# Last state-space stage of a decoder kernel: causal mask as a minimum on VectorE, exponential in place, score products on GpSimd

## What is computed

```python
zxbcdt = hidden_states @ W_in               # z: 4096, x: 4096, B: 128, C: 128, dt: 64
xbc = silu(causal_conv1d(xbc, conv_w) + conv_b)      # 4 taps
dt = softplus(dt + dt_bias)
dA_cs = cumsum(dt * A, axis=tokens)
diff = dA_cs[i] - dA_cs[j]                  # per sequence, per head, 128x128
L = exp(where(j <= i, diff, -inf))
Y = einsum('bcign,bcjgn,bcijgh,bcjghp->bcighp', C, B, L, dt * x)
y = (Y + D * x) * silu(z)
out = (y * rsqrt(mean(y * y) + eps) * norm_w) @ W_out
```

## Time and profile before

| | |
|---|---|
| median of 3 runs | 1987.97 us (1985.36 to 1990.80) |
| profiled execution | 1988.18 us |
| its span, first to last instruction | 1986.4 us |
| TensorE busy | 1718.8 us, 87% of the span |
| VectorE busy | 1181.7 us, 59% |
| ScalarE busy | 922.8 us, 46% |
| GpSimd busy | 443.1 us, 22% |
| mean granted TensorE clock | 0.945 of full |
| the loop over pairs | about 1200 to 1625 us of the span |

### The profile page before, as it was taken

The page is one execution under the profiler, slowest core; times in us unless marked ns, Lnnn a source line. Parts: engine busy times, 40 slices in busy tenths (PEclk is TensorE's granted clock), DMA queues, the critical chain, the costliest instruction groups (busy, mean ns, idle before and its releaser), DMA issues. The chain is left out here.

```text
span 1986.4 us, 37376 instructions
## 1 busy us (share of the span) xinstructions
PE 1718.8 (87%) x13974; PEld 1341.0 (68%) x13974; DVE 1181.7 (59%) x2340; ACT 922.8 (46%) x1876; POOL 443.1 (22%) x497
## 2 busy tenths in 40 slices
PE   7976756789999899977667878999999997999898
PEld 4765643469999755653456756777777785888666
DVE  3675568556555622225653477888888865666632
ACT  2344466336655521212144355667667653555432
POOL 1020010123333131221300123445455441000200
PEclk9998977899999999998779899999999998999999
DMA  2020000401000082221000000101011003111000
GB/s 97 2 88 2 3 29 1 138 9 33 24 24 24 19 354 39 46 32 63 13 1 3 26 25 17 33 24 32 25 31 32 24 16 118 33 32 32 1 1 22
DMA packets 27104, 77.86 MB, mean 39 GB/s; under 512 B 2928, under 2 KB 14832, under 8 KB 24560
## 3 DMA queue, kind: packets, MB, share of 16 engines
q1 hardware_dynamic: 22912, 71.17, 10.5%
q0 software_dynamic: 4080, 5.13, 1.6%
HBM read 63.01 MB, written 13.28 MB: 38 GB/s over the span
## 5 line engine op out<-in xcount | busy, mean ns | idle before, releaser
L2446 DVE SCALAR_TENSOR_TENSOR arena<-bank,arena 128x508 f32<-128x508 f32 (+2 forms) x204 | 151.5, 743 | 28.5 <-ACT arena L2442 16.1
L217 PE MATMUL bank<-const 128*128 128x256 f32 (+1 forms) x244 | 101.7, 531 | 37.2 <-PEq L65 37.2
L2572 PE MATMUL bank<-L3a_wo,L3a_y_gated 128*128 128x256 f32 x512 | 124.0, 386 | 0.0
L2800 DVE TENSOR_TENSOR L3a_decays<-L3a_decays,L3a_cb_masked 128x512 f32<-128x512 f32 x128 | 94.7, 802 | 44.0 <-ACT L3a_decays L2684 44.0
L2684 ACT ACTIVATE L3a_decays<-bank 128x512 f32<-128x512 f32 x128 | 66.1, 604 | 98.1 <-PE bank L2546 98.1
L2599 PE MATMUL bank<-L3a_xnT_high,L3a_w_high 128*128 128x512 f32 x256 | 106.3, 415 | 1.5 <-ACT L3a_decays L2684 1.5
L2572 PEld LDWEIGHTS bank<-L3a_wo,L3a_y_gated 128*128 128x128 f32 x512 | 92.4, 190 | 17.5 <-issue 7.3
L2599 PE MATMUL bank<-L3a_xnT_high,L3a_w_low 128*128 128x512 f32 x256 | 100.6, 393 | 0.0
L2599 PE MATMUL bank<-L3a_xnT_low,L3a_w_high 128*128 128x512 f32 x256 | 100.4, 392 | 0.0
L217 PEld LDWEIGHTS bank<-const 128*128 128x128 f32 x244 | 44.1, 208 | 64.4 <-issue 64.4
L1863 PE MATMUL bank<-L1f_experts,xnT 128*128 x184 | 84.6, 603 | 2.3 <-DVE xnT L1965 2.3
(11 more groups left out here) (592 smaller groups left out, 4762.5 us busy)
## 6 DMA issues: line engine op xcount, KB each, us to landing
arena<-in_L3p SPq DMA_DIRECT2D x32, 388.0 KB, 3.0
L1f_experts<-in_L1f SPq DMA_DIRECT2D x8, 1536.0 KB, 17.3
arena<-in_L1x SPq DMA_DIRECT2D x18, 384.0 KB, 3.0
arena<-in_L3x SPq DMA_DIRECT2D x18, 384.0 KB, 3.0
arena<-in_L0f SPq DMA_DIRECT2D x1, 4224.0 KB, 13.8
arena<-in_L3f SPq DMA_DIRECT2D x1, 4055.0 KB, 12.8
rows_sent<-L1a_blank SPq DMA_DIRECT2D x1, 2967.0 KB, 11.2
xnT<-rows_sent SPq DMA_DIRECT2D x23, 129.0 KB, 2.0
```

The lines of the kernel that those rows point to most:

```text
L217: self.nc.tensor.matmul(self.k.ps[bank][:, 0:width], self.k.ident, self.k.const[:, 0:width], start=True, stop=True)
L2446: return nc.vector.scalar_tensor_tensor(dst[:, :, d:], psum[:, :, 0:P - d], wcol, dst[:, :, d:], ALU.mult, ALU.add)
L2572: mm = nc.tensor.matmul(ps[g // 2][:, (g % 2) * C:(g % 2 + 1) * C], yg[:, o, g * P:(g + 1) * P], wo[:, o, :], start=False, stop=False, ski ...
L2800: nc.vector.tensor_tensor(d, d, cbm[:, 4 * half:4 * half + 4, :].rearrange("p b t -> p (b t)"), ALU.mult).then_inc(S["dec_ready"], 1)
```

## The change

- The mask leaves TensorE: `later`, `ident_r` and the four mask matmuls are gone, and each difference matmul starts its bank itself.
- VectorE's `bound` takes the place of `weigh`: for each of four banks the minimum of the differences in PSUM and `highest`, a 128x128 table (1e30 where allowed, -1e30 elsewhere) repeated for four sequences, written to `dec` in SBUF. It now gives `diff_read`, and waits for `y_psum` where the exponentials did.
- ScalarE's exponentials run in place in `dec`, after `diff_read`, and give the new `exp_ready`.
- `weigh` moves to GpSimd, to the end of its pass, behind the sum of squares; the first pair's is done in pass 1, ahead of the second's.

```diff
--- before.py
+++ after.py
@@ -2413,7 +2413,7 @@
         da_src = da[:, :, :].rearrange("p (f m) (a q h) -> p f m a q h", f=2, q=2, h=2)
         dax_dst = dax[:, :, :].rearrange("p a (h f r q m) -> p a h f r q m", h=2, f=2, r=4, q=2)
         ROWS = [[(h, f, r) for h in range(2) for f in range(2) for r in own] for own in ((0, 1), (2, 3))]
-        identr, later = st.sb("ident_r", [P, P], F32R), st.sb("later", [P, 4, P], F32R)
+        highest = st.sb("highest", [P, P])
         lrow = st.sb("diff_left", [P, 2, P], F32R)
         rrow = st.sb("diff_right", [P, 4, P], F32R)
         dec = st.sb("decays", [P, 2, 2, NB, P])
@@ -2425,7 +2425,7 @@
         S = {n: st.sem(n) for n in (
             "dt_psum", "zdt", "abs_dt", "exp_dt", "exp1_dt", "log_dt", "bc_psum", "bc_first", "bc_conv",
             "bc_ready", "cb_psum", "cb_ready", "da_ready", "z_psum", "x_psum", "z_read", "x_scaled", "x_read",
-            "x_conv", "x_ready", "xt_psum", "xt_read", "diff_psum", "diff_read", "dec_ready",
+            "x_conv", "x_ready", "exp_ready", "xt_psum", "xt_read", "diff_psum", "diff_read", "dec_ready",
             "y_psum", "y_read", "y_ready", "pair_small", "wo_ready", "out_done", "sq_ready", "sq_added",
             "ms_psum", "zero_set", "dve_step", "d_ready", "x_high", "x_low", "w_high",
             "w_split", "dA_rows", "dA_rows_act", "cs_psum", "cs_copy", "cs_high", "cs_merged", "cs_left", "cs_rows", "steps_ready", "slot_read", "mask_set")}
@@ -2539,12 +2539,9 @@
                             pe.wait_ge(S["xt_read"], j * 2 - 1 + n)
                         else:
                             pe.wait_ge(S["y_read"], j * 2 - 5 + n)
-                        nc.tensor.matmul(bank("d", n)[:, :], identr[:, :], later[:, :, :].rearrange("p m t -> p (m t)"),
-                                         start=True, stop=False)
-                    for n in range(4):
                         g = slice(32 * n, 32 * n + 32)
                         nc.tensor.matmul(bank("d", n)[:, :], lrow[g, s, :], rrow[g, :, :].rearrange("p m t -> p (m t)"),
-                                         start=False, stop=True).then_inc(S["diff_psum"], 1)
+                                         start=True, stop=True).then_inc(S["diff_psum"], 1)
 
                 def make_y(pe, j, o):
 
@@ -2630,7 +2627,6 @@
 
                 pe.sem_inc(S["out_done"], SLOT_FREE)
                 pe.wait_ge(S["x_low"], 1)
-                pe.wait_ge(S["mask_set"], 2)
                 passes(pe, pair, tail)
 
             @block.scalar
@@ -2678,11 +2674,9 @@
                 def exponents(act, j, s):
                     d4 = dec[:, s, :, :, :].rearrange("p h b t -> p (h b t)")
                     for n in range(4):
-                        act.wait_ge(S["diff_psum"], j * 4 + n + 1)
-                        if not early(j):
-                            act.wait_ge(S["y_psum"], j * 2 - 2)
-                        nc.scalar.activation(d4[:, n * HALF:(n + 1) * HALF], bank("d", n)[:, :],
-                                             ACT.Exp).then_inc(S["diff_read"], 1)
+                        act.wait_ge(S["diff_read"], j * 4 + n + 1)
+                        d = d4[:, n * HALF:(n + 1) * HALF]
+                        nc.scalar.activation(d, d, ACT.Exp).then_inc(S["exp_ready"], 1)
 
                 def squares(act, j, o):
 
@@ -2738,8 +2732,7 @@
                 ln.vector(dve)
                 step = Chain(dve, S["dve_step"])
                 nc.vector.memset(zero[:, :], 0.0).then_inc(S["zero_set"], 1)
-                nc.vector.tensor_copy(identr[:, :], k.ident).then_inc(S["mask_set"], 1)
-                nc.vector.tensor_copy(later[:, :, :], over(k.c["causalT"], 4)).then_inc(S["mask_set"], 1)
+                nc.vector.tensor_scalar(highest[:, :], k.c["causalT"], 2.0, BIG, ALU.mult, ALU.add).then_inc(S["mask_set"], 1)
                 dve.wait_ge(S["x_high"], 1)
                 nc.vector.tensor_tensor(xl[:, :, :], xnT[:, :, :], xh[:, :, :].bitcast(F32),
                                         ALU.subtract).then_inc(S["x_low"], 1)
@@ -2791,15 +2784,16 @@
                         nc.vector.tensor_scalar(csl[:, t], csl[:, t], rows[:, 2:3], rows[:, 3:4], ALU.mult,
                                                 ALU.add).then_inc(S["cs_rows"], 1)
 
-                def weigh(dve, j, s):
+                def bound(dve, j, s):
 
                     for n in range(4):
                         h, half = n // 2, n % 2
-                        d = dec[:, s, h, 4 * half:4 * half + 4, :].rearrange("p b t -> p (b t)")
-                        dve.wait_ge(S["diff_read"], j * 4 + n + 1)
-                        nc.vector.tensor_tensor(
-                            d, d, cbm[:, 4 * half:4 * half + 4, :].rearrange("p b t -> p (b t)"),
-                            ALU.mult).then_inc(S["dec_ready"], 1)
+                        dve.wait_ge(S["diff_psum"], j * 4 + n + 1)
+                        if not early(j):
+                            dve.wait_ge(S["y_psum"], j * 2 - 2)
+                        nc.vector.tensor_tensor(dec[:, s, h, 4 * half:4 * half + 4, :],
+                                                bank("d", n)[:, :].rearrange("p (b t) -> p b t", b=4),
+                                                over(highest[:, :], 4), ALU.min).then_inc(S["diff_read"], 1)
 
                 def skip(dve, j, o):
 
@@ -2826,7 +2820,7 @@
                     first = is_first(j)
                     step.restart()
                     if not first:
-                        weigh(dve, j, s)
+                        bound(dve, j, s)
                     for half in range(2):
                         dve.wait_ge(S["x_scaled"], j * 2 + half + 1)
                         p3 = bank("x", half)[:, :].rearrange("p (b t) -> p b t", b=4)
@@ -2849,7 +2843,8 @@
                                                 bank("t", half)[:, :].rearrange("p (b h d) -> p b h d", b=4, h=2),
                                                 along(dtc[:, s, bs, :], HD), ALU.mult).then_inc(S["xt_read"], 1)
                     if first:
-                        weigh(dve, j, s)
+                        dve.wait_ge(S["mask_set"], 1)
+                        bound(dve, j, s)
                     else:
                         gate(dve, j, 1 - s)
 
@@ -2894,6 +2889,18 @@
                     pool.wait_ge(S["sq_ready"], j + 1)
                     nc.gpsimd.tensor_tensor(sqsum, sqsum, ysq, ALU.add).then_inc(S["sq_added"], 1)
                     pool.wait_ge(S["sq_added"], j + 1 + SLOT_FREE)
+
+                def weigh(pool, j, s):
+
+                    if is_first(j):
+                        pool.wait_ge(S["cb_ready"], 2)
+                    for n in range(4):
+                        h, half = n // 2, n % 2
+                        d = dec[:, s, h, 4 * half:4 * half + 4, :].rearrange("p b t -> p (b t)")
+                        pool.wait_ge(S["exp_ready"], j * 4 + n + 1)
+                        nc.gpsimd.tensor_tensor(
+                            d, d, cbm[:, 4 * half:4 * half + 4, :].rearrange("p b t -> p (b t)"),
+                            ALU.mult).then_inc(S["dec_ready"], 1)
 
                 def scale_output(pool, j, s):
 
@@ -2934,6 +2941,10 @@
                         pool.sem_inc(S["slot_read"], 2)
                     if not early(j):
                         add_squares(pool, j - 2)
+                    if not is_first(j):
+                        if is_second(j):
+                            weigh(pool, 0, 0)
+                        weigh(pool, j, s)
 
                 def tail(pool):
                     scale_output(pool, N - 1, 1)

```

## The result

The changed kernel took 2018.3 us (median of four executions, 2016.6 to 2021.2) against 1988.2 for the kernel before (four, 1985.4 to 1990.8), a ratio of 1.0153 with a 95% interval of 1.0134 to 1.0172: 30 us, or 1.5%, slower. The profiled execution took 2017.31 us. The forecast was 2013.7, slower.

What follows compares the result with a forecast made beforehand. TensorE, busy 353 of 355 us, was taken to set the pace. Circle +1, gate stalls +28.5, start and end -4 gave +25.5 on 1988.18: 2013.7 us; likeliest case 1995 to 2034, full range 1985 to 2034.

Steps and rivals of the forecast that it cites:

- TensorE's gain: Dropping four mask matmuls frees 0.87 us a pass on TensorE, 26 us over 30 passes, if nothing else needs longer.
- The minima and exponentials: VectorE's minima from PSUM at 0.682 us each, starts 0.60 apart; ScalarE's in-place exponentials at 0.62.
- The circle: Minima, exponentials, squares, x scaling, taps, gates, next minima: 13.72 us against 13.69, so +1 us over 30 passes.
- the first x scaling behind the squares: Rival: x scaling need not await the squares' full time on ScalarE, TensorE paces at 12.8 us, 1958 us; chance 0.10.
- GpSimd's products: Four 128x512 score products on GpSimd at 1.09 us each, starts 1.05 apart, bounds 1.04 and 1.27.
- a pause of 0.51 before the steps: On GpSimd ahead of even passes, a 0.51 us gap after the products, then two steps from 11.4 to 13.0.
- The stall of the gates: VectorE's gates take turns with GpSimd's SBUF reads: 0.6 us before odd passes, 1.3 before even, +28.5 us; chance 0.76.
- full exclusion: Alternative at VectorE's gates: one behind a whole GpSimd operation costs 1.04 us, making the sum 3 us more.
- The start: First two passes, where nothing covers TensorE, and the end: masks gone and taps earlier, together -4 us.
- The sum: Whole kernel: +1, +28.5 and -4 give +25.5 us on 1988.18, so 2013.7 us.
- What would show it: Trace signs: period near 14.6 us, TensorE waits of 0.5 or more, gates near 1.1, taps' wait 2.3, output scaling 0.61.
- the fourth rival: GpSimd's weight split comes late and holds TensorE: 0.5 us every other pass, +7.5, 2021 us; counted inside the 0.76 case.

Runs made afterwards that it cites:

- the third experiment: The kernel before with its four mask matmuls and their preparation left out, exponential scaled by 1e-4: 1956.1 us, ratio 0.9831.
- the first experiment: The changed kernel with the four score products left out, minima and exponentials as changed: 1985.4 us, ratio 0.9982.
- the sixth experiment: The changed kernel with ScalarE's squares moved behind the second z activation, GpSimd's work reordered and the score products left out: 1961.8 us, ratio 0.9846.

## Why the prediction was right, and where it was short

- **TensorE's gain.** "0.87 us" a pass: 0.91 by the third experiment. Right, and right too that it would not arrive.
- **The minima and exponentials.** 0.682 taken, 0.675 measured; 0.62 taken, 0.632 measured.
- **The circle** of 13.72 us: the first experiment shows just that. The forecast rests on this step, and on its statement that it costs the whole gain. What could be done about it the prediction had only as a rival (the first x scaling behind the squares): the sixth experiment shows that moving the squares brings the period within 0.08 us of TensorE's 12.78.
- **GpSimd's products.** Taken at 1.09, measured at 1.275 (4.97 for four, instead of 4.2). This is the mis-sized term; it stood in the text as the bound of 1.27. Ahead of odd passes it moves the splits back by some 0.75 us: the high split starts 11.67 after the minima, not 10.9. Ahead of even passes most of that is met by a second error. The prediction put a pause of 0.51 before the steps, as in the earlier trace rows, but they follow the products without one, and only 0.17 stands between the addition and the products: the steps start at 11.66 instead of 11.4.
- **The stall of the gates.** Predicted 0.6 ahead of odd passes and 1.3 ahead of even ones. From the first gate to the next minima is 1314.04 - 1311.92 = 2.12 and 1329.24 - 1326.52 = 2.72, where 1.20 is free: 0.92 and 1.52, on average 1.22 instead of 0.95. The mechanism was the right one, as the runs with products left out (no stall), moved (free ahead of odd passes) and with writes in place of reads (no stall) show. But ahead of odd passes it does not strike where the prediction had it: the low split, which comes later, begins under the first gate, and it is the second gate that stalls (1.58, with 0.69 for the first), where the prediction had the first wait 0.6 and the second go free. Ahead of even passes it strikes as worked out: 0.67 at the first gate (0.45 predicted, the steps being later) and 0.85 at the second (0.85), by the starts 1326.52, 1327.79 and 1329.24, less 0.60 each. By full exclusion my even pass would have cost 1.49, with 1.04 at the second gate. The sum of 1.52 does not tell the two apart, since the phase had moved as well, but the 0.85 at the second gate is the figure of the earlier trace rows and not 1.04.
- **The start.** Predicted -4. From pass 0's first x transposes to pass 2's it took 1225.93 - 1181.88 = 44.05 us and takes 1220.20 - 1179.93 = 40.27: -3.8.
- **The sum.** From pass 2's transposes to the final sum of squares it was 1636.34 - 1225.93 = 410.4 us and is 1666.00 - 1220.20 = 445.8, +35.4. That is 29 passes at 14.93 - 13.69 = 1.24, less half a microsecond; I had taken 30. With the start, the stage is 31.6 us longer. The profiled executions differ by 29.1: outside the stage the two differ by 2.5 us the other way, within the 5 us over which runs of one kernel scatter. Some 2 us of that lie ahead of the stage, where the code is the same: its first instruction starts at 1158.23 before and at 1156.26 now. So 8 us of larger stalls (29 x 0.27) were met by a pass counted too many (1.2), the end and that scatter, and the forecast came out 3.6 us under the profiled run. That it came so near is in part luck: the stalls alone were 8 us too small.
- **What would show it.** Period "near 14.6 us, alternating by pass": 14.93, by turns 14.67 and 15.20. Gates "near 1.1": 1.29 by the mean. Taps' wait "about 2.3": 2.31. Output scaling "down to 0.61": 0.61. Waits of TensorE "of half a microsecond or more" before the z activation's y matmuls: up to 1.4. The waits for GpSimd, the fourth rival (a split that comes late), are there too, at 0.43 and 0.29 ahead of even passes. What they cost by themselves was not separated; together they are under the 1.52 us of stall in the same pass, and the minima that close the circle start right behind the gates, without waiting for them.

## What to carry to other kernels

Before work is taken off the engine that is busiest, close the circle of the others (who waits for whom from one pass to the next) and write its length beside the pace: here it was 13.72 against 13.69, so the gain of 0.9 us a pass was gone before anything was added. Turning the order of two engines round (ScalarE then VectorE into VectorE then ScalarE) is an edit of the schedule, to be followed by a new place for what queued behind, here the squares. And work given to an idle GpSimd costs by what it and its followers read while VectorE runs instructions with two SBUF inputs: lay its reads under instructions that read PSUM, and the same products cost 8 us (1969.4 against 1961.8 without them) instead of 33 (2018.3 against 1985.4).

## What the runs showed of the hardware

- A two-input operation over 128x512 on GpSimd that writes over one of its inputs takes 1.27 to 1.30 us by the median, in either order of operands, with either output type, as a product or a difference (1.257 at the least, of 128 in each of seven runs), while a subtraction of two such inputs into a third buffer takes 1.09 and the addition of a broadcast zero 1.04.
- Taking turns is not a matter of length: a copy of 16 columns goes from 0.20 to 0.66 us and a one-column addition from 0.19 to 0.52 beside two-input work on VectorE; memsets of 512 columns in the same place take 0.51 to 0.56 in the loop, beside a gate or not, and hold nothing up (gates 0.684).
- When the two engines alternate (changed kernel, ahead of even passes), a GpSimd operation of 1.04 grows to 1.49, and the gates of 0.684 to 1.34 and 1.52. One operation in GpSimd's row before a gate is enough: ahead of odd passes it is 0.69 for the first and 1.58 for the second.
